# Moving the last group's scores and values ahead of the first expert rows, and GpSimd's root of the gate's norms ahead of its normalisation

## The reference

```python
h = layernorm(x) * (1 + ca) + sa
x = x + ga * block_attention(h)      # 8 heads, blocks of 32 rows, features elu(q proj) + 1
h = layernorm(x) * (1 + cb) + sb
x = x + gb * expert_ffn(h)

# block_attention, per head and block of 32 rows
num = qp @ (kp.T @ v);  den = qp @ kp.sum(rows);  out = num / den;  out @ w_out.T + b_out

# expert_ffn: each row goes to one of 8 experts
wg_n = wg / max(norm(wg, axis=1), 1e-4)
gates = softmax(x @ w_red @ wg_n.T);  idx = argmax(gates);  score = gates[idx]
y = gelu(x @ w1[idx] + b1[idx]) @ w2[idx] + b2[idx];  out = y * score
```

## Time and profile before

| | us |
|---|---|
| median of 3 runs | 271.66 (271.24 to 271.77) |
| profiled execution, its own time | 270.44 |
| its span | 268.7 |
| busy: TensorE, VectorE, ScalarE, GpSimd | 246.0, 223.3, 182.4, 156.7 |
| mean granted TensorE clock | 0.983 |

### The profile page before, as it was taken

How to read it: one execution, slowest core, us unless ns; L and a number is a source line. 1 busy time by engine, 2 the same in 40 slices (tenths; PEclk the granted TensorE clock), 3 DMA queues, 4 the chain that set the end, 5 groups by cost and what they waited for, 6 DMA issues and landing times.

```text
span 268.7 us, 11525 instructions
## 1 busy us (share of the span) xinstructions
PE 246.0 (92%) x4010; PEld 179.8 (67%) x4011; DVE 223.3 (83%) x743; ACT 182.4 (68%) x485; POOL 156.7 (58%) x196
## 2 busy tenths in 40 slices
PE   7899979999999999999999889998899999999960
PEld 3354555665765756656656556787788999999950
DVE  6778799999999999999999999698975776666740
ACT  2865657777787776877877664848967766767730
POOL 4323235165188488496680865887789874554550
PEclk9999999999999999999999998999999999999995
DMA  6820001954507217022040052414655454444300
GB/s 176 258 50 2 2 4 43 277 149 124 164 18 205 99 50 241 34 92 72 4 132 34 2 164 84 139 51 138 210 167 167 120 135 136 113 114 130 111 22 0
DMA packets 21583, 28.44 MB, mean 106 GB/s; under 512 B 3343, under 2 KB 16531, under 8 KB 21536
## 3 DMA queue, kind: packets, MB, share of 16 engines
q1 hardware_dynamic: 17920, 19.26, 26.2%
q0 software_dynamic: 3296, 8.41, 8.7%
q10 hardware_dynamic: 320, 0.13, 0.2%
HBM read 15.38 MB, written 10.64 MB: 97 GB/s over the span
## 4 chain that ended last, share of the span: by engine, by line
PE 51%; DVE 19%; issue 7%; ACT 4%; POOL 3%; SPq 1%; DMA 1%; ACTq 1%; POOLq 1%; DVEq 0%
PE ps L897 11%; PE ps L980 10%; PE ps L1009 10%; DVE phi L1287 9%; PE ps L908 5%; PE ps L861 5%; PE ps L937 2%; PE ps L922 2%; ACT ebuf L642 2%; PE ps L930 2%; PE ps L974 2%; DVE qk L1182 1%; POOL out L576 1%; DVE h L1340 1%; PE ps L850 1%
## 5 line engine op out<-in xcount | busy, mean ns | idle before, releaser
L642 ACT ACTIVATE ebuf<-ps 128x512 f32<-128x512 f32 x128 | 69.5, 595 | 30.6 <-PE ps L897 30.5
L1287 DVE SCALAR_TENSOR_TENSOR phi<-ebuf,ps 128x512 f32<-128x512 f32 x128 | 81.2, 676 | 2.1 <-ACT ebuf L642 1.8
L897 PE MATMUL ps<-qk,proj_w 64*128 64x512 f32 x384 | 62.2, 429 | 4.8 <-DVE phi L1287 4.1
L713 ACT ACTIVATE gT<-ps,b_cols 128x128 f32<-128x128 f32 x156 | 44.5, 368 | 17.1 <-PE ps L980 14.4
L1009 PE MATMUL ps<-w_sb,gT 128*128 x312 | 42.1, 278 | 3.3 <-ACT gT L713 1.4
L897 PEld LDWEIGHTS ps<-qk,proj_w 64*128 64x128 f32 x384 | 31.5, 186 | 15.7 <-DVE phi L1287 4.2
L1009 PEld LDWEIGHTS ps<-w_sb,gT 128*128 128x128 f32 x312 | 37.9, 192 | 4.9 <-issue 4.8
L576 POOL DMA_INDIRECT out<-yo,tok x27 | 27.1, 1004 | 22.0 <-DVE yo L1597 20.3
L511 POOL DMA_INDIRECT sorted_rows<-rec,pos x32 | 32.7, 1022 | 8.2 <-issue 7.2
L908 PEld LDWEIGHTS ps<-phi 128*32 128x32 f32 x2048 | 23.3, 112 | 19.0 <-issue 13.9
L908 PE MATMUL ps<-phi 128*32 128x32 f32 x2048 | 29.7, 199 | 0.2 <-ACT a_sb L655 0.2
(11 more groups left out here) (212 smaller groups left out, 426.6 us busy)
## 6 DMA issues: line engine op xcount, KB each, us to landing
rin<-sorted_rows SPq DMA_DIRECT2D x39, 192.5 KB, 2.5
vbd<-vals SPq DMA_DIRECT2D x32, 68.0 KB
w1b<-in_L_ffn_w SPq DMA_DIRECT2D x4, 512.0 KB
w_sb<-in_L_ffn_w SPq DMA_DIRECT2D x8, 256.0 KB
sorted_rows<-pad_rec SPq DMA_DIRECT2D x9, 192.5 KB, 5.6
x_all<-in_L_attn_x SPq DMA_DIRECT2D x2, 256.0 KB, 3.5
w1b<-in_L_ffn_b SPq DMA_DIRECT2D x1, 512.0 KB
sorted_rows<-rec,pos POOLq DMA_INDIRECT x32, 3.0
```

The costliest lines, as they stand in the source:

```text
L642: nc.scalar.activation(ebuf[:, h % 2, j, :], x_ps[h % 2][:, j, :], ACT.Exp, scale=1.0 / SHRINK, bias=math.log(SHRINK) - 1.0).then_inc(s_ex ...
L713: last = nc.scalar.activation(gT[:, b, c_, :], h_ps[b][:, j, i * P:(i + 1) * P], ACT.Gelu, bias=b1_cols[:, bass.ds(e * FC + c_, 1)])
L897: last = mm(x_ps[h % 2][:, j, :], proj_w[rows, w_part, h, :], qk_of(g, part, h // HT)[rows, :], start=w_part < part, stop=w_part == part)
L1287: last = v.scalar_tensor_tensor(out=phi[:, h % 4, j, :], in0=ebuf[:, h % 2, j, :], scalar=SHRINK, in1=x_ps[h % 2][:, j, :], op0=ALU.min, o ...
```

## The change

Three edits. On TensorE and ScalarE the last group's scores and values go ahead of the first slot's rows, and the load of the gelu table goes ahead of the first slot's copy. `Y_APART` is 3 in place of 5, so the fourth slot (`s` = 3) is the first that writes the second bank and the first that waits for `s_lgs`. On GpSimd the root of the gate's norms, with its wait, goes ahead of `norm1_apply(2)`.

```diff
-    Y_APART = 5
+    Y_APART = 3
@@ GpSimd, step
+                if isinstance(g, int) and g == 0:
+                    pool.wait_ge(c_wg, 3)
+                    rsqrt(wg_n[:, 2:3], wg_n[:, 1:2], c_wgr)
                 if nxt:
                     norm1_apply(g + 2)
                 if prev3:
                     scatter(g - 3, [2])
-                if isinstance(g, int) and g == 0:
-                    pool.wait_ge(c_wg, 3)
-                    rsqrt(wg_n[:, 2:3], wg_n[:, 1:2], c_wgr)
@@ ScalarE
             keep_a(NG - 1, H - 2, False)
+            nc.scalar.activation(warm[:, :], neg_half[:, 0:1], ACT.Gelu).then_inc(f_table, 1)
             act.wait_ge(s_early, 2)
             act.wait_ge(l_exp, 16 * (3 * E // 2 + 2))
             keep_in(0, 0)
-            nc.scalar.activation(warm[:, :], neg_half[:, 0:1], ACT.Gelu).then_inc(f_table, 1)
+            keep_a(NG - 1, H - 1, False)
             keep_in(1, 1)
-            keep_a(NG - 1, H - 1, False)
             gelu(0, 0)
@@ TensorE
             pe.wait_ge(s_vs, NG)
+            keep_busy(2, t_ps)
+            scores(NG - 1, H - 2)
+            keep_busy(2, t_ps)
+            apply_values(NG - 1, 0, False)
             pe.wait_ge(s_early, 2)
-            keep_busy(3, t_ps)
             slot_in(0)
-            scores(NG - 1, H - 2)
-            apply_values(NG - 1, 0, False)
+            scores(NG - 1, H - 1)
             slot_hidden(0)
             slot_in(1)
-            pe.wait_ge(s_asb, H * NG - 1)
-            pe.wait_ge(s_on, 2 * (NG - 1))
-            keep_busy(2, ps[:, 4, :])
-            scores(NG - 1, H - 1)
+            apply_values(NG - 1, 1, False)
             slot_hidden(1)
-            apply_values(NG - 1, 1, False)
             slot_in(2)
```

## The result

| | before | after |
|---|---|---|
| median, us | 271.67 (270.50 to 271.94, 6 executions) | 269.17 (268.49 to 269.51, 6) |
| profiled execution, its own time | 270.44 | 268.49 |
| its span | 268.7 | 266.7 |
| busy: TensorE, VectorE, ScalarE, GpSimd | 246.0, 223.3, 182.4, 156.7 | 245.3, 223.3, 182.7, 157.6 |
| mean granted TensorE clock | 0.983 | 0.983 |

The ratio is 0.9908, with an interval of 0.9884 to 0.9931. The forecast was 269.5, range 268.9 to 270.5. The profiled execution became 1.95 us shorter, the median 2.50; the forecast was 2.15 for both. That the two differ is the main thing the experiments explain.

What follows compares the result with a forecast made beforehand. Bounds: GpSimd's late root in the first pass, slot 0's row load at the join, then VectorE, ScalarE and TensorE. Terms -1.7 and -0.45 give -2.15: profiled 270.44 to 268.3, median 271.66 to 269.5, range 268.9 to 270.5.

Steps and rivals of the forecast that it cites:

- The root's term: First pass, GpSimd: the gate norms' root ahead of group 2's layernorm ends VectorE's 2.06 us stall; -1.7 us.
- Rival 2: First pass: the root's early lead is mostly given back in TensorE's dense stretch after 35 us; 270.2 to 271.0, chance 0.08.
- The join: Where the two parts meet: last group's scores and values ahead of slot 0's rows bring later work forward; -0.45 us.
- From there VectorE, ScalarE and TensorE hand the time on: Behind the last group's centering: the join's gain passes to the end, scatters and late slots' loads moving along; -0.45 us kept.
- The bank: Second bank from the fourth slot: TensorE's 1.31 us wait at `outer(4)` only moves one product later; 0 us.
- Rival 1: At the join: `hidden(0)` a microsecond later, so no gain or a little loss; 269.85 to 270.3, chance 0.16.
- Rival 3: At the join: gelu table load blocks twice as long, costing about 0.4; sum 270.35, chance 0.05.
- Rival 4: TensorE's stretch from 198.76 us: granted clock falls, making it slower than before, such as 272.2; chance 0.04 including unseen waits.
- Rival 5: At the join: slot 0's gelu register read overlaps fully, gaining 0.6 to 1.0; 268.9 to 269.35, chance 0.11.

Runs made afterwards that it cites:

- either mend: Changed kernel with the gelu table load behind slot 0's copy: 268.61 us; changed kernel without GpSimd's second filler memset: 268.57 us; both at once: 268.66 us.

## Why the prediction was right, point by point

- **The root's term was right in its place and its mechanism.** Head 4's `phi` at 26.78 (forecast 26.77), TensorE's wait 0.53 (0.44), and the lead of 1.66 at head 7 of the last pass; at the transposes of the first seven groups it is 1.66 to 1.69. Rival 2, that it is given back in TensorE's dense stretch, fell. The agreement to hundredths holds for these two executions: in the two profiles of the root alone it is 0.91 and 1.55 at head 7.
- **The same term was mis-sized for the median.** It was read off one execution, in which the clock did not fall behind TensorE's 1.49 us. In others it does, and the move, by shortening that idle time to 0.53, takes the fall away as well: 2.8 for the root alone instead of 1.7. The scaling from the profile to the median, "0.5% above that execution", hid it: the 1.22 us between the two were not a share that stays. Afterwards they are 0.68, and -0.06 and 0.42 where the changed kernel ran again (268.44 against 268.50 for its profile, 268.47 against 268.05). In those two comparisons the change gave 3.60 and 3.28 in the median, and 268.44 and 268.47 lie below the forecast's range of 268.9 to 270.5. So that the first measurement, 269.17, lies in it is in part luck: the mechanism forecast is there, but a second one of about a microsecond was not foreseen.
- **The join was right to a few hundredths up to the centering.** In times of before: `hidden(0)` 169.45 (forecast 169.45), the second `apply_values` 170.62 (170.58), `outer(0)` 172.91 (172.7 to 172.95), the projection 173.90 (173.66 to 173.92). The residual is 173.33 against 175.19, so 1.86, 0.20 beyond the shared 1.66 (0.07 to 0.32); the centering 0.44 beyond it (0.36 to 0.61).
- **"From there VectorE, ScalarE and TensorE hand the time on" was the step that failed**, together with the scatters that were to move along. Of 0.44 the last scatter kept 0.20: the memset cost `lden` most of the difference, and without it the last scatter is 0.51 ahead of before (26.67 to 27.18). At `outer(10)` 0.45 is ahead again (35.89 to 35.44), since in this execution SP's load followed the scatter 0.14 sooner (4.80, not 4.94) and `outer(10)` waited 0.18 for its gelu where it had waited 0.55 at its own issue. In the span, 268.7 to 266.7, 0.3 of the join is left. So the profiled gain is 1.95 where the sum was 2.15.
- **The bank: 0, as forecast.** `outer(4)` waits 0.54 for its gelu, not for VectorE, and `hidden(6)` starts at 187.93, in times of before 189.59 against 189.83, which is the join's 0.20 to 0.27 at this point and no more.
- **The other rivals.** Rival 1 (the join gives nothing) and the forecast's 0.45 can't be told apart at the end: 0.53 in one comparison, within the spread. Rival 3 fell by ScalarE's rows. Rival 4's mechanism is real, but in the kernel before: its clock falls behind the idle time that the change shortens, not behind 198.76 us. Rival 5 needed a gelu whose register read overlaps; it started 0.89 behind the copy ahead of it again (169.07 to 169.96), as in the earlier trace rows.

## What to carry to other kernels

A small instruction that stands behind a long wait in an in-order program is worth moving as soon as its own input is there earlier and something lies idle for it; follow the gain to the engine that is late next: here that gave 1.69 us where 1.66 was measured in one pair of profiles, though another execution of the same edit was only 0.91 ahead. Shortening an idle time of TensorE can be worth more than the idle time: compare several executions of the kernel before, and where they spread over a per cent, look for a stretch that one trace shows at the lower clock and another doesn't. An early lead in front of a load that waits for scattered rows to land can be lost there: here the stretch from the last scatter to the load varied by 1.1 us between profiles.

## What the runs showed of the hardware that was not expected

- The same idle time of 1.49 us, at the same place of the same instructions, was followed by a granted clock of 1.00 in one execution and of 0.50 in another; there the two groups of products behind it took 1.79 and 1.65 us instead of 1.16 and 0.96. Filling the idle time with products of no use made the kernel 1.26 us faster in the median.
- A memset of GpSimd, which reads nothing, more than doubled a VectorE `tensor_scalar` of 128x32 beside it: 0.37 instead of 0.17 us.
- The time from the start of the last scatter to the load that waits for it was 4.7 to 5.8 us from one profile to the next, a spread of 1.1 us, which is more than the join or either mend could bring.
